# Sums of squares of q and k from the high and low BF16 halves of the squares, both read in place

## What is computed

```python
def softmax_kernel(data, proj, is_query):
    d = data.shape[-1]
    data_normalizer = d ** (-0.25)
    ratio = proj.shape[0] ** (-0.5)
    data_dash = jnp.einsum('bhnd,md->bhnm', data_normalizer * data, proj)
    diag = jnp.sum(data * data, axis=-1, keepdims=True) * 0.5 * data_normalizer ** 2
    if is_query:
        m = jnp.max(data_dash, axis=-1, keepdims=True)
    else:
        m = jnp.max(data_dash, axis=(-3, -2, -1), keepdims=True)
    return ratio * (jnp.exp(data_dash - diag - m) + EPS)
...
q_prime = softmax_kernel(q, proj_mat, is_query=True)
k_prime = softmax_kernel(k, proj_mat, is_query=False)
```

## Time and profile before

| | us |
|---|---|
| median of 3 runs | 1719.46 |
| lowest and highest of the runs | 1717.51, 1719.79 |
| the profiled execution: its time | 1719.79 |
| the profiled execution: its span | 1719.8 |
| PE busy | 1582.3 (92%) |
| DVE busy | 1137.4 (66%) |
| ACT busy | 680.8 (40%) |
| POOL busy | 409.8 (24%) |
| chain that ended last, PE's share | 72% |
| chain that ended last, DVE's share | 18% |
| L1006, matmuls: first and last start | 383.9, 574.1 |

### The profile page before, as it was taken

The page is one execution under the profiler, slowest core; times in us unless marked ns, Lnnn a source line. Parts: engine busy times, 40 slices in busy tenths (PEclk is TensorE's granted clock), DMA queues, the critical chain, the costliest instruction groups (busy, mean ns, idle before and its releaser), DMA issues.

```text
span 1719.8 us, 25185 instructions
## 1 busy us (share of the span) xinstructions
PE 1582.3 (92%) x9743; PEld 1199.8 (70%) x9809; DVE 1137.4 (66%) x2618; ACT 680.8 (40%) x1359; POOL 409.8 (24%) x251
## 2 busy tenths in 40 slices
PE   3989999999989889999999999998999999986987
PEld 2556666555655568888888888888888976666664
DVE  6678664104565999999987697668765833785223
ACT  3420001122232466777667764346534621441110
POOL 3788888888300000000000000000000000002331
PEclk9989999999999999999999999999999999996999
DMA  9335535454652413224320254335413224545941
GB/s 358 82 59 119 113 79 124 62 92 74 191 183 87 143 46 114 87 91 127 109 70 28 83 172 167 102 118 191 139 39 95 85 71 153 212 180 208 317 151 50
DMA packets 194889, 213.67 MB, mean 124 GB/s; under 512 B 81359, under 2 KB 149597, under 8 KB 194770
## 3 DMA queue, kind: packets, MB, share of 16 engines
q1 hardware_dynamic: 118146, 187.01, 33.0%
q0 software_dynamic: 75760, 22.70, 8.3%
q10 hardware_dynamic: 864, 2.36, 0.4%
HBM read 144.74 MB, written 68.40 MB: 124 GB/s over the span
## 4 chain that ended last, share of the span: by engine, by line
PE 72%; DVE 18%; ACT 3%; issue 3%; DMA 3%; SPq 0%; POOLq 0%; POOL 0%; ACTq 0%; DVEq 0%
PE bank L1075 18%; PE bank L905 13%; PE bank L906 13%; PE bank L904 12%; DVE junk L1480 4%; PE bank L1245 4%; PE bank L1233 3%; PE bank L1129 2%; DVE eb L1515 2%; DVE eb L1524 2%; PE bank L1101 1%; PE bank L1144 1%; PE bank L1006 1%; PE bank L1114 1%; PE bank L914 1%
## 5 line engine op out<-in xcount | busy, mean ns | idle before, releaser
L1075 PE MATMUL bank<-hb,eb 128*128 128x193 f32 (+3 forms) x2400 | 417.4, 331 | 13.3 <-ACT node L1922 7.1
L1075 PEld LDWEIGHTS bank<-hb,eb 128*128 128x128 f32 (+3 forms) x2400 | 400.2, 190 | 23.8 <-issue 10.2
L2119 POOL DMA_INDIRECT table<-amount,place x170 | 344.6, 2027 | 70.1 <-issue 49.1
L2125 POOL IOTA iota8i<- 128x8 int32 x1 | 0.1, 140 | 957.0 <-DMA node_rows<-node 957.0
L1515 DVE SCALAR_TENSOR_TENSOR eb<-shift_b,as_low,shift_b 128x640 f32<-128x640 f32 (+1 forms) x240 | 196.3, 860 | 0.3 <-PE bank L1075 0.2
L1908 ACT ACTIVATE eb<-eb,asd 128x640 f32<-128x640 f32 (+1 forms) x240 | 181.3, 811 | 28.7 <-DVE eb L1515 28.7
L1480 DVE CUSTOM_DVE_ANT_0 junk<-ab,absent 128x1250 bf16<-128x1250 f32 x120 | 174.3, 1452 | 1.6
L1524 DVE SCALAR_TENSOR_TENSOR eb<-eb,count 128x1280 f32<-128x1280 f32 (+1 forms) x120 | 174.4, 1453 | 0.2 <-ACT eb L1908 0.2
L904 PE MATMUL bank<-w_o_hi,aT_hi 128*128 128x384 bf16 (+1 forms) x360 | 119.2, 331 | 0.0
L904 PE MATMUL bank<-wg_hi,x1T_hi 128*128 128x384 bf16 (+3 forms) x360 | 119.0, 331 | 0.1
L905 PE MATMUL bank<-w_o_lo,aT_hi 128*128 128x384 bf16 (+1 forms) x360 | 118.9, 330 | 0.0
(11 more groups left out here) (290 smaller groups left out, 2967.7 us busy)
## 6 DMA issues: line engine op xcount, KB each, us to landing
w<-in_w SPq DMA_DIRECT2D x16, 1152.0 KB, 13.1
shift_b<-shift_rows SPq DMA_DIRECT2D x24, 625.0 KB, 5.8
h_rows<-h_row SPq DMA_DIRECT2D x27, 388.0 KB
hb<-h_rows SPq DMA_DIRECT2D x12, 873.0 KB
ar<-node_rows SPq DMA_DIRECT2D x27, 384.0 KB, 3.2
table<-zero POOLq DMA_DIRECT2D x3, 3054.0 KB, 19.1
tab<-table SPq DMA_DIRECT2D x27, 312.5 KB, 3.4
qk_rows<-qk_row SPq DMA_DIRECT2D x12, 625.0 KB
```

The lines of the kernel that those rows point to most:

```text
L1075: ins = T.matmul(bank[w // 2][0:M, c0:c0 + GC + 1], p[0:K, u, w * P:w * P + M], hv[0:K, t, 0:GC + 1], start=opens and u == 0 and w % 2 == ...
L2119: G.indirect_dma_start(tables[i], bass.IndirectOffsetOnAxis(place[:, c:c + 1], axis=0), amount16[:, c:c + 1], None, compute_op=ALU.add).th ...
```

## The change

`halves` becomes BF16. The squares stay where they are, as FP32 words in `sq`. A BF16 view of the same bytes (`sq_parts`, columns by two) gives the upper 16 bits of each word at index 1, which are the square cut to BF16. DVE subtracts this from the FP32 square and writes the rest, rounded to BF16, over the lower 16 bits (index 0). PE then sums both parts: for each tile of nodes two BF16 matmuls, whose stationary operand has a step of two elements (4 bytes) between columns, accumulate in the same two PSUM columns. PE's wait for `qk_square` becomes one for the new semaphore `square_lo`; the wait for `qk_square` goes to DVE, in front of the subtraction.

```diff
-v_set v_mm v_copy v_out0 v_out1 qk_mm qk_square qk_hi qk_lo norm_mm diag_in qk_out0 qk_out1 top_mm k_max top_v top_pe
+v_set v_mm v_copy v_out0 v_out1 qk_mm qk_square square_lo qk_hi qk_lo norm_mm diag_in qk_out0 qk_out1 top_mm k_max top_v top_pe
...
-        ident, zero, ones, halves = put("ident", [128, 128]), put("zero", [128, D]), put("ones", [128, 128]), put("halves", [128, 2])
+        ident, zero, ones, halves = put("ident", [128, 128]), put("zero", [128, D]), put("ones", [128, 128]), put("halves", [128, 2], BF16)
...
+        sq_parts = [s[:, :].bitcast(BF16).rearrange("p (n w) -> p n w", w=2) for s in sq]
...
             def norms(m):
                 c0, c1 = chunk(m)
                 pe.wait_ge("pool_set", 8)
-                pe.wait_ge("qk_square", m + 1)
+                pe.wait_ge("square_lo", m + 1)
                 pe.wait_ge("diag_in", m)
                 for j in range(-(-(c1 - c0) // P)):
                     R = rows(c0 // P + j)
-                    ins = T.matmul(bank[3][0:R, 2 * j:2 * j + 2], sq[m % 3][:, j * P:j * P + R], halves[:, :],
-                                   start=True, stop=True)
+                    for part in (1, 0):
+                        ins = T.matmul(bank[3][0:R, 2 * j:2 * j + 2], sq_parts[m % 3][:, j * P:j * P + R, part], halves[:, :],
+                                       start=part == 1, stop=part == 0)
                 ins.then_inc(sem["norm_mm"], 1)
...
             def qk_split(m):
                 c0, c1 = chunk(m)
                 dst = qk_out[m // NC % 2]
+                w = c1 - c0
+                ve.wait_ge("qk_square", m + 1)
+                V.tensor_tensor(sq_parts[m % 3][:, 0:w, 0], sq[m % 3][:, 0:w], sq_parts[m % 3][:, 0:w, 1],
+                                ALU.subtract).then_inc(sem["square_lo"], 1)
                 ve.wait_ge("qk_hi", m + 1)
```

## The result

The changed kernel took **1712.47 us** (median of 9 runs, 1705.33 to 1717.2), the kernel before beside it 1719.46 (9 runs, 1717.51 to 1724.53): ratio 0.9957, interval 0.9943 to 0.9971, so 7.0 us less. The forecast was 1711.2, in a range of 1705.5 to 1722.0. On a second chip the same text took 1713.61 against 1718.94 (0.9968, 0.9952 to 0.9984), 5.3 us less.

A forecast was written before the change was run, and what follows sets the result against it. PE was taken to bound 380 to 463.3 and 534.4 to 559 us, a ring of waits between, DVE afterwards. Terms -7.1 + 0.5 + 0.45 - 2.5 + 0.4 = -8.25 us gave 1711.2 us, range 1705.5 to 1722.

The forecast's parts named there:

- rivals A and B: A: strided passes stay near 0.10 us, 1721.7, chance 0.13; B: they take twice that, near 1737, chance 0.08.
- The passes: PE's sums of squares: 0.028 us a BF16 pass, saving 0.6 us per full chunk and 0.1 per short one.
- Stretch 1: 380 to 463.3 us, bound by PE: sums of 11 full and 5 short chunks save 7.1 us.
- The tables: Counting tables, loaded after POOL's last scatter, land near 457 to 458.6 us; their date costs +0.5 us on the path.
- The delay by the subtractions: New DVE subtractions hold back scatters that start inside them, making the last some 1.5 us later.
- The ring: Chain of ACT and DVE waits, 463.3 to 534.4 us: six full-chunk turns grow 0.2 us each, +1.2.
- chunk 25: Its sums, on the chain at half clock, start 0.65 us later and shrink from 1.83 to 0.43: -0.75 together.
- Rival C: PE idles longer in the ring stretch; one more half-clock piece costs 3.6 us, giving 1714.8; chance 0.15.
- Stretches 3 and 4: 534.4 to 559 us, PE leads: -2.5 us; 559 to 577 us, DVE leads: +0.4 us.
- Rival D: More is saved: the ring doesn't grow, tables don't wait, the half-clock piece is missed: 1705.9 us, chance 0.06.

The follow-up runs named there:

- c1: The changed kernel once more, unaltered, on the second chip: 1713.61 us, ratio 0.9968 to the kernel before.
- c5: The changed kernel with the last 8 of 170 scatters left out, so the tables can be loaded early: 1708.52 us.
- a1: The changed kernel without the subtraction; PE sums the upper halves twice in the same number of BF16 passes: 1706.87 us.
- a2: The changed kernel with its subtraction and the wait for it, but PE multiplies the FP32 squares as before: 1720.07 us.
- a4: The kernel before, with ACT's copy of a counted tile put behind the next chunk's square and high part: 1704.01 us.
- a3: The changed kernel, with ACT's copy of a counted tile put behind the next chunk's square and high part: 1699.94 us.
- c3: The changed kernel with the subtraction on GpSimd from chunk 18 on and ACT's copy behind the square and weight copy: 1697.27 us.
- d3: As c3, but the additions of the tables begin one chunk later: 1696.7 us.

## Why the prediction was right, and where it wasn't

The sum was -8.25 us; the pieces of one profile make -7.5, the medians -7.0 and -5.3. The mechanism held, and rivals A and B fell with the first rows. That the first measurement came within 1.3 us of the forecast is luck in part: two terms were off by more than 1 us, in opposite directions.

**The passes.** Predicted 0.22 us for a full chunk, measured 0.21 and 0.22. The choice between 0.028 and 0.10 us, by the row of the same type against the row with the same operand, was right, and the page's rule that would have made it rival A (the Trainium skill, TensorE: Matmul & The Clock Gate, section LDWEIGHTS) doesn't hold here: a BF16 pass takes 0.027 us with the 4-byte step too, an FP32 one 0.10.

**Stretch 1.** -7.1 predicted, -7.3 in the profile, and within 0.1 the same in c1 and c5. A short chunk's passes save 0.17 us, where I took 0.1.

**The tables, the term that was mis-sized.** "I take +0.5 us on the path"; the wait was 2.9 and 4.7 us, and 5.1 by medians in c5. The step that failed was to read two dates from one execution as if they were fixed. From PE's first sums to the last scatter it was 64.1 us there (383.92 to 448.03), the shortest of all thirteen executions with all scatters (64.1 to 73.5). In the profiled execution after, the tables landed by 458.57, inside the 457 to 458.6 of the forecast; but PE's first sums came 2.4 us earlier, so DVE was ready at 455.6 and not at 458.2. In c1 both moved, the sums to 382.44 and the last scatter to 450.68. The delay by the subtractions, which I did weigh, came out as priced (1.7 us, where I had 1.5). With the mean date of the four kernels without it, 450.8, the same working would have given about +3.

**The ring.** +1.2 for six turns at 0.2 us, and -0.75 for chunk 25. Turn by turn, four turns grew by 0.12 or 0.13 us, the fifth by 0.24 and the others by nothing: +0.7 in all. The last turn, behind the sums of chunk 25, fell from 9.2 to 7.5 us: -1.7. So the stretch got shorter by 1.0 us instead of longer by 0.45. PE's later sums (9.2 us of waits in 4 for the subtraction; the fifth wait of the list lies behind the ring) are off the path but for what they do to the clock. Rival C's piece didn't come on top: there were two pieces at half clock before, at 497 to 501 and 518 to 525 us, and two shorter ones after, at 491 to 495 and 512 to 516. Where such a piece falls goes with up to 1.5 us a turn: c1 had none in its fifth turn (8.7 instead of 10.2 us) and a longer one beside its last (8.6 instead of 7.5). That its whole stretch still took 63.9 us, like the 64.2 after, is luck of this kind, and so is part of the -1.0.

**Stretches 3 and 4.** -2.5 and +0.4 predicted, -2.6 and +0.5 measured. The subtraction took 0.73 and 0.40 us where I had 0.69 and 0.38, and its successor stood 0.62 us behind (506.36 less 505.74) as taken.

**The subtraction as a whole.** B says 2 us (a1), where the forecast had +1.2, +0.65 and +0.4. a2, with the costs and without the gain, was forecast as rival A at +2.3: its B was 2.8 us longer than the kernel before's (114.3 against 111.5), the stage with A 4.2 (197.1 against 192.9), and yet its median 0.6 shorter, interval -0.15% to +0.2%. It doesn't refute 2.3 us, nor does it show them.

**What I read wrong in the experiments.** That a4 would gain only 3 to 7 us from the moved copy, and that the change would be worth 9 to 12 beside it (the medians have 4.1 and 7.1). I had priced the ring by its turns alone; with the copy moved the clock is 1.00 over the whole stretch, so the pieces at half clock went away together with the ring's pauses, and I count them to its price. And I hadn't asked which engine is full once PE is not.

**The base.** The sum was set against 1719.8 us. That is the span; the 1719.79 beside it belongs to another execution, since 1.7 us lie around a span. So the profiled execution took about 1721.5 and stood 2 us above the median, not 0.3. The forecast isn't touched by it: it is the median less the sum, 1719.46 - 8.25 = 1711.2. Rival D's time is 1705.9 by its own sum, while the range starts at 1705.5; nothing hangs on the 0.4 us.

## What to carry to other kernels

With two moving columns a pass cost 0.10 us in FP32 and 0.027 in BF16, and two BF16 passes over the halves of an FP32 word, read in place, cost about a quarter of one FP32 product; the price is one subtraction on another engine. Before such a gain is booked, look what date the next stage waits for, and take its distance from your own engine's date from several executions: one profile had the shortest of thirteen, and 3 to 5 of the 7.3 us went that way. And where a stretch has no full engine, look for the ring first: moving one copy behind one square gave 17 us to the kernel before, more than twice what the cheaper products gave.

## What the runs showed of the hardware that I had not expected

- A stationary BF16 operand with a step of 4 bytes loads as fast as a packed one: eight passes of 128 columns in 0.21 us.
- The date of a string of 170 scatters varies by 6.4 us (448.03 to 454.47) between executions of kernels that issue it alike, the spread is there thirty scatters before the end (375.15 to 382.14), and PE's date doesn't follow it.
- What lengthens a scatter is where it starts. From 370 us on, in all fourteen traces, the 390 that started outside a DVE `tensor_tensor` of two SBUF operands took 1.99 to 2.01 us; of the 89 that started inside one, 60 took more than 2.05, up to 2.78 us.
- Pieces of 3 to 7 us at a granted clock of 0.50 (the lower of TensorE's two levels, 1.2 and 2.4 GHz) began in or right behind pauses of PE of 2.35 and 2.66 us before, 3.17 and 3.44 after, some for its sums and some for DVE's maximum; after pauses of 2.04 and 2.31 us in the same trace the clock stayed at 1.00. In a3 and a4 PE's longest pauses were 1.63 and 0.35 us and the granted clock was 1.00 throughout the stretch.
- A GpSimd subtraction of 512 columns takes 1.04 us where DVE takes 0.73. DVE's additions of 1250 columns go from 0.80 to between 1.04 and 1.46 us when they start while one runs (the 1.46 in c3, 1.05 to 1.19 in d3).
